# The evacuation of the K projection moved from VectorE to ScalarE in a fused attention and feed-forward kernel

## The reference

```python
def attn(x, wq, wk, wv, wo):       # q, k, v = x @ w.T in blocks of 256 tokens
    scores = einsum('bhjqd,bhjkd->bhjqk', q, k2) / sqrt(64)   # k2: previous and own block
    attn = softmax(where(band & kpos_ok, scores, min), axis=-1)
    return einsum('bhjqk,bhjkd->bhjqd', attn, v2).reshape(B, S, D) @ wo.T
def ffn(x, theta, phi, theta_noise, phi_noise):
    real = x @ cos(theta + theta_noise)
    imag = x @ sin(phi + phi_noise)
    return sqrt(real * real + imag * imag)
x = x + layernorm(attn(layernorm(x), wq, wk, wv, wo))
x = x + layernorm(ffn(layernorm(x), theta, phi, theta_noise, phi_noise))
```

## Time and profile before

| | |
|---|---|
| median of the two runs | 4197.12 us (4192.48 and 4201.76) |
| profiled execution | 4201.76 us, span 4200.2 us on core 1, the slowest |
| the other cores | spans from 4170.4 us |
| PE busy | 3293.7 us, 78% of the span |
| DVE busy | 1706.3 us, 41% |
| ACT busy | 1154.6 us, 27% |

### The profile page before, as it was taken

One profiled execution on the slowest core, in us unless ns is written; L12 is line 12 of the kernel. 1 busy time (PEld: TensorE's weight loads), 2 busy tenths in 40 slices (PEclk: granted clock), 3 DMA queues, 4 the chain that ended last, 5 costly groups with the idle time before them and its releaser, 6 DMA issues.

```text
span 4200.2 us, 51721 instructions; the slowest of 8 cores (4170.4 to 4200.2 us)
## 1 busy us (share of the span) xinstructions
PE 3293.7 (78%) x19808; PEld 2144.5 (51%) x19808; DVE 1706.3 (41%) x3728; ACT 1154.6 (27%) x1920; POOL 111.7 (3%) x215
## 2 busy tenths in 40 slices
PE   0028887979888797988878798888879788887975
PEld 0016555555555555555555455555555555555552
DVE  2324345162634526263352516254360725436162
ACT  3423132231403223041322314141231414123141
POOL 1100000000000000000000000000000000000000
PEclk6557988889888898988889797988889898888977
DMA  6773331414233151423315141422414142241413
GB/s 204 244 256 121 121 141 56 185 54 146 83 121 141 50 191 42 149 90 121 141 43 198 61 175 47 161 101 86 155 61 161 61 161 101 81 161 61 161 51 130
DMA packets 54161, 511.24 MB, mean 122 GB/s; under 512 B 5792, under 2 KB 5920, under 8 KB 28576
## 3 DMA queue, kind: packets, MB, share of 16 engines
q0 software_dynamic: 30384, 266.35, 16.7%
q1 hardware_dynamic: 23536, 241.58, 16.4%
HBM read 465.97 MB, written 41.94 MB: 121 GB/s over the span
## 4 chain that ended last, share of the span: by engine, by line
PE 61%; DVE 24%; issue 5%; DMA 4%; ACT 4%; DVEq 1%; POOL 0%; ACTq 0%; SPq 0%; POOLq 0%
PE pb L504 33%; PE pb L456 13%; PE pb L654 5%; DVE attn_sb L685 5%; DVE stats L682 4%; PE pb L754 4%; PE pb L644 2%; DVE ao_sb L792 2%; PE pb L716 2%; DMA wsc<-pl 2%; PE pb L401 1%; DVE sc L332 1%; DVE attnT_sb L727 1%; DVE fml L424 1%; ACT L311 1%
## 5 line engine op out<-in xcount | busy, mean ns | idle before, releaser
L682 DVE TENSOR_REDUCE stats<-pb 128x1 f32<-128x384 f32 (+2 forms) x512 | 269.1, 526 | 875.6 <-PE pb L654 875.6
L754 PE MATMUL pb<-v_sb,attnT_sb 128*128 128x64 f32 x2880 | 472.6, 306 | 84.6 <-DVE attnT_sb L727 83.2
L754 PEld LDWEIGHTS pb<-v_sb,attnT_sb 128*128 128x128 f32 x2880 | 430.8, 223 | 160.2 <-issue 157.6
L456 PE MATMUL pb<-fmh,slot0h 128*128 128x256 bf16 x1024 | 279.9, 273 | 269.5 <-DMA slot0l<-wsc 269.5
L696 ACT ACT_TABLE_LOAD x256 | 328.4, 1283 | 583.5 <-DVE attn_sb L685 583.2
L456 PE MATMUL pb<-fmh,slot1h 128*128 128x256 bf16 x960 | 292.4, 305 | 159.1 <-DVE sc L825 86.8
L504 PE MATMUL pb<-slot2h,fmh 128*128 128x512 bf16 x992 | 375.9, 379 | 13.4 <-ACT ao_sb L882 13.4
L504 PE MATMUL pb<-slot2h,fml 128*128 128x512 bf16 x992 | 375.9, 379 | 0.0
L504 PE MATMUL pb<-slot2l,fmh 128*128 128x512 bf16 x992 | 375.9, 379 | 0.0
L414 ACT ACT_TABLE_LOAD x32 | 41.1, 1283 | 1167.5 <-PE pb L401 1167.5
L685 DVE TENSOR_SCALAR attn_sb<-pb,stats 128x384 f32<-128x384 f32 (+2 forms) x512 | 303.6, 593 | 55.3 <-DVE stats L682 0.5
(11 more groups left out here) (113 smaller groups left out, 4632.1 us busy)
## 6 DMA issues: line engine op xcount, KB each, us to landing
slot0h<-wsc SPq DMA_DIRECT2D x33, 2048.0 KB, 10.2
slot1h<-wsc SPq DMA_DIRECT2D x33, 2048.0 KB, 13.0
slot0l<-wsc POOLq DMA_DIRECT2D x33, 2048.0 KB, 12.9
slot1l<-wsc POOLq DMA_DIRECT2D x33, 2048.0 KB, 15.1
slot2h<-wsc SPq DMA_DIRECT2D x33, 2048.0 KB, 11.8
slot2l<-wsc POOLq DMA_DIRECT2D x33, 2048.0 KB, 14.0
x_sb<-x POOLq DMA_DIRECT2D x32, 512.0 KB, 6.2
y<-sc POOLq DMA_DIRECT2D x32, 512.0 KB, 3.9
```

Of the source, the lines that this page charges most:

```text
L456: ins = tensor.matmul(pb[b][:, 0:256], lhsT, rhs, start=(n_mm == 0), stop=(n_mm == 23))
L682: ev[f"mx_{g}_{uu}"] = ve.inc(vector.reduce_max(stats[:, P + up:P + up + 1], kept, axis=AX.X))
L754: ins = tensor.matmul(pb[b_av][:, (h % 8) * DH:(h % 8 + 1) * DH], lhsT, rhs, start=(first_in_bank and ci == 0), stop=(last_in_bank and ci ...
```

## The change

The K projection's last argument becomes "s", so its eight evacuations per block are activations with Copy on ACT (L473) instead of copies on DVE (L471). The guards of banks 0 to 3 then hold an event of ACT's counter. Since the scores on PE waited for K only through DVE's order (K's copies come ahead of Q's), a wait for ACT's last K evacuation is added ahead of them. Lines after 641 are one higher in the changed kernel.

```diff
@@ emit_kvq
             emit_proj_fm(gg, base_use, k_sb, bufg * 2048, f"kp_{gg}",
-                         h_ev, l_ev, "v")
+                         h_ev, l_ev, "s")
@@ pair_scores_t
                 def _(tensor, u=u, specs=specs):
                     kb.wait(tensor, ve, ev[f"qp_{g}_done"])
+                    kb.wait(tensor, ac, ev[f"kp_{g}_done"])
                     kb.bank_wait(tensor, [specs[0][0], specs[1][0]])
```

## The result

The changed kernel takes 1.0017 times the time of the kernel before, with a 95% interval of 1.0009 to 1.0025: no faster, and if anything 7 us slower. The profiled execution took 4206.35 us, with a span of 4204.8 us on core 3, the slowest. The forecast was 36 us faster, 4166 us. In some executions of any of these kernels four or all eight cores show a lower granted clock and take some per cent longer, so all times, spans and blocks from here on are of executions, or of halves of the chip, without that.

What follows compares the result with a forecast made beforehand. TensorE was taken to set the time except where it waits for VectorE, 72.4 us of it for K copies. Restart 20 + clock 0 + rhythm 16 = 36 us off 4201.8 gave 4166 us, range 4144 to 4192.

Steps and rivals of the forecast that it cites:

- Step 1: First K copy behind the third layernorm's square root: one table load, no drain; TensorE restarts 1.3 us earlier, 20 us overall.
- Step 2: Later K copies on ACT take 1.7 us against 2.62 us per matmul group: no second hole, cost nothing.
- Step 3: DVE sheds eight K copies, 3.4 us a block, but waits for the V projection anyway: worth nothing.
- Step 4: TensorE's clock in the K projection's second half: no change taken, ends -2.1 and +0.7 us a block.
- Step 5: The shift breaks the repeating clock pattern that lies badly for attention: 1.2 us for each of 13 blocks, 16 us.
- A: Only the K projection's hole shrinks and the clock pattern forms again as badly: 4182 to 4192, say 4185 us; chance 0.22.
- C: Slower: clock returns no sooner (0.66 us lost), each block's last stretch 1.46 us longer; 12 us more, 4214; chance 0.08.
- D: A table load holds ACT twice its row (2.57 us), so TensorE restarts as now: 4200 us; chance 0.04.
- E: No table load ahead of the K copies: 56 us gained, 4145 us; chance 0.02.
- B: Clock stays up through the shorter hole or returns sooner, attention keeps its good pattern: 51 us gained, 4151; chance 0.17.

Runs made afterwards that it cites:

- one_section: Changed kernel with a block's eight K copies in one ScalarE section, 16 table loads instead of 128: blocks of 245.69 us, spans 4181 to 4206 us, no whole-chip time.
- fill_hole: Changed kernel with 14 unused matmuls in the hole ahead of group 5 of the K projection: 4164.62 us.
- the V runs: Changed kernel with 4 or 8 matmuls left out of each V projection, or 4, 8, 12 or 16 added (-1.73 to +3.46 us): slowest spans 4143.8 to 4261.2 us.
- v_less_4: Changed kernel without 4 matmuls of each V projection (-0.86 us a block): blocks 240.7 to 241.8 us, slowest core's span 4143.8 us.

## Why the prediction was wrong

Step 1 (restart) was right to 0.01 us, its load and its copy too. The hole gave 1.35 us a block, 15 x 1.35 = 20 us, as the sum has it. The two rules that were weighed there, both of the Trainium skill's page "ScalarE: Activation LUTs" (sections Table sets and What ACT_TABLE_LOAD costs, so one page and not two), would each have given the wrong restart: a copy behind a square root does have a load here (one_section shows that the load goes with the section, whatever the copy would need), and the copy follows it 0.01 us later, with no drain.

Step 2 (pace) was right: the second half is busy throughout (13.18 of 13.18 us), and one_section shows that the loads there cost nothing.

Step 3 (VectorE's gain is worth nothing) agrees with the V copies, which wait for TensorE as before; no run tested it by itself.

Step 4 (clock behind the hole) was mis-sized: I took no change, with +0.7 as an end. It was +0.62, 9 us in all, so nearly half of the 1.35 us was lost where it was gained. The case behind that end is what happened: the clock rose at the same moment as before, counted from the square root (7.65 and 7.80 us), and the part gained at the front was run at half clock.

Step 5 (rhythm) failed, and with it the forecast. It was to give 16 us and gave nothing; in its place another 0.62 us a block, 9 us, went in the stretches outside of the K projection. The microsecond or more by which everything was to move was never there: behind the K projection 0.62 us was left of it, and by the next block nothing. "That pattern can't repeat unchanged" was argued from this shift; but the pattern did repeat, with its pieces moved by some tenths, and every core went into it from block 1 or 2. I took the good lengths (242.7, 243.3) as what a block has off the pattern, and counted the change as a way off it. The better reading was that 245.80 us, four times over in the earlier trace rows, is a length to which blocks return from other lengths, so that the default for a small saving is nothing. The trace of before has it on all eight cores: the first blocks are 242.1 to 243.2 and then 244.5 to 244.7 us long, and all that follow in that sequence 245.7 to 245.9. The runs bear this out, with its limits: at -0.86, -1.73 or +0.86 us the blocks do leave it. Which of the two happens depends on amounts of less than a microsecond, and I can't work it out from the trace of before.

Of the rivals, A (4182 to 4192) had the idea that the pattern forms again, but not that it takes all; C had the sign, and its first price (0.66 of the 1.32 lost behind the hole) was right, its second (1.46 us in the last stretch) came to 0.40; that the measured 4206 us lies between D (4200) and C (4214) bears out neither sum. D fails by the copy that follows its load at once, E by the 128 loads. B's clock that stays up shows only in fill_hole. The range missed since I had kept 0.66 us a block as the least gain in A, though the trace showed lengths, not gains, to be what repeats.

Shown: slower matmuls take back the hole's gain (the stretches of the two kernels), the slow clock behind the hole comes from idle time in it (fill_hole), blocks can settle at lengths 3.4 us apart (the V runs), the loads are free (one_section). Not shown: why the changed kernel settles at 245.7 where both 0.86 us less and more do not. No run tested this, and the cause stays open.

## What to carry to other kernels

In a loop that repeats to 0.1 us while the clock of TensorE falls and rises in it, don't price a saving by its own length: a saving of 1.3 us gave nothing, one of 0.9 us elsewhere gave 4 to 5, and added work of 1.7 us cost nothing. Try such a change with a few sizes of dummy work beside it, or the verdict is on the alignment and not on the change. And go for the whole hole rather than a quarter of it: moving the consumer's order (the K projection ahead of a layernorm) removed it on either engine, and where the hole stayed, unused matmuls in it kept the clock up.

## What was not expected of the hardware

The length of a block is not monotone in its work: 240.7 to 241.8 us at 0.86 us less, 245.69 in the changed kernel, 243.0 to 244.6 at 0.86 us more. Steady blocks are 238.93, 242.32, 245.75 and 249.16 us long, 3.4 us apart, in four of these kernels, while equal work gave 244.81 and 239.13 us in two blocks in a row (v_less_4) at a granted clock of 0.87 and 0.91. That the steps are equal fits the Trainium skill's page "TensorE: Matmul & The Clock Gate", Part 1, which says that the gate's activity windows run freely and are not restarted by the kernel: a pattern can then repeat only if the block keeps step with them. The runs agree with that; none tests it by itself.
